# Products of the probabilities with the value rows: one product of 512 columns for P's high half, sums kept unweighted in PSUM's two banks

## The chip, the cores and the metric

The kernel runs on one core of a Trainium2 chip. The metric is the time of one execution on the device in microseconds (us), lower is better. The core has a matrix engine (PE, TensorE), a vector engine (DVE), an activation engine (ACT), a general engine (POOL, GpSimd) and a queue engine (SP) that here issues almost all DMAs. PE writes its sums to PSUM, which has eight banks of 512 f32 columns on 128 partitions; all the others read and write SBUF, and DVE and ACT read PSUM.

## The reference, cut to what matters

One layer of attention on a graph of 4096 nodes with 256 features, after a layer norm:

```
h  = max(layernorm(x), 0)
lQ = masked_x @ Wlq ;  lK = h @ Wlk ;  lV = h @ Wlv + blv
local = where(adj, lQ @ lK.T / 16, -1e9)
le, ge, ee = exp(local - m), exp(global - m), exp(es - m)
denom = sum(le) + ge + ee
res = le/denom @ lV + ge/denom * gV + ee/denom * eV
out = x + max(res, masked_x)
```

`global` and `es` are one number per row, `gV` is one row of 256 values, and `eV = masked_x @ Wev + bev` has a row for each node.

## The kernel before

**Tiling.** The 4096 query rows are taken as 16 row pairs n = 0..15, each of two tiles t = 0, 1 of 128 rows. The 4096 keys are taken as four groups g of 1024. A step p = 4n + g is one block of 2 x 128 rows by 1024 keys. In each step PE makes the scores of block p, and, some six steps later, the products of that block's probabilities with the value rows. All matrix factors are split into a high and a low half in f16, and three of the four products of halves are made: with P the probabilities and V the value rows, P_high·V_high (L1107), P_high·V_low (L1109) and P_low·V_high (L1111), each of 256 columns. `v_rows[:, kc]` holds V_high and V_low of a chunk of 128 keys side by side in 512 columns.

**Order on PE.** It is written out by hand. Up to step 11 a step has four score products (`classic`, banks ps_w, ps_v and twice ps_x) with four chunks of P times V behind each. From step 12 on the scores are made by seven smaller products (`p1`, `p7`, `p5`, `p6`, `p4`, `p2`, `p3`, three instructions of 512 columns each) in a fixed mix with the 16 chunks of P times V. `p_times_v(p, first, last_one)` counts chunks i = 0..15 of step p. Chunks 0 to 7 belong to unit u = 2(p-6)-1 (tile t = 1 of block p-7), chunks 8 to 15 to u + 1 (tile t = 0 of block p-6). So a row pair n opens with chunk 8 of step 4n + 6, its tile t = 0 ends with chunk 15 of step 4n + 9, and its tile t = 1 ends with chunk 7 of step 4n + 10.

**The accumulators.** ps_u has two banks. Row pair n sums into bank n % 2, tile t into the columns t·256 to t·256 + 255. The next row pair uses the other bank, and only from n = 2 on does PE wait for DVE to have read the bank (`s_c1`, from L1100). The last row pair's tile t = 1 sums into ps_w. `ps_u[:, 1, 0:2]` also holds a small sum in step 6 (L1308).

**The other engines' lists** are written out by hand too, step by step. DVE takes the scores out of PSUM (L1476, L1507, L1513, L1519), and has the work that closes a row pair n: `weights` in step 4n + 9, `side_rows` in step 4n + 10 (L1572 and L1575: r12 = blv + w_g·gv + w_e·bev, twice, once per tile), `es_rows` and `local_rows` in step 4n + 11 (L1602; L1587: t_sb = ps_u·r_u + r12), `row_top` in step 4n + 12. ACT makes the masks (L777), the exponentials (L790) and P_high (L814). POOL makes P_low (`p_low`, L611), the low halves of the queries (L596, L591), and the last sum of a row pair (`finish`, L621). SP issues in its own list the transposes of P (L376, L378) and, in step 4n + 13, the store of row pair n (L434). For block slots in SBUF, DVE's take-out of step p waits for the low half of block p-5 (`s_plo`).

Of the kernel before, what the change touches and what calls it, by code (L numbers as in the profile page):

```python
# [24 lines left out]
def build(nc, x, adj, mxT, mx, WlqT, WlkT, Wlv, blv, WgqT, WgkT, Wgv, bgv, Wes, Wev, bev, out):  # L25
# [26 lines left out]
    with ExitStack() as ctx:  # L52
# [6 lines left out]
        def sem(name):  # L59
# [13 lines left out]
        ps_xrow = ps_gv  # L73
        ps_norm = ps_x[:, 0, D:D + 1]
# [111 lines left out]

        eye16 = sb("eye16", [P, 2, P], F16)
# [39 lines left out]
        s_den, s_w, s_e, s_c1, s_c2, s_r, s_fin = (  # L227
            sem(n) for n in ("s_den", "s_w", "s_e", "s_c1", "s_c2", "s_r", "s_fin"))
# [82 lines left out]
        def scale_steps(n):  # L311
            return 3 * min(n, 1) + 3 * min(n, QH) + 5 * max(n - QH, 0)

# [193 lines left out]
        def _(pool):  # L507
# [105 lines left out]

            def finish(n):
# [22 lines left out]
            for p in range(4, NPER + LAG_E):  # L637
# [11 lines left out]
                if live:  # L649
                    p_low(u + 1)  # L650
                if p % NG == 3 and QH <= (p + 5) // NG < NP:
                    mx_low((p + 5) // NG)
# [268 lines left out]
        def _(pe):  # L921
# [156 lines left out]
            def p_times_v(p, first, last_one):  # L1078

                for i in range(first, last_one):  # L1080
# [6 lines left out]
                    if j == 0:  # L1087
# [3 lines left out]
                        if u == LAST + 1:  # L1091
                            pe.wait_ge(s_o11, NPER)
# [9 lines left out]
                    if u >= LAST and t:  # L1102
                        acc = ps_w[:, 0:D]
                    opens = kc == 0 and (t == 0 or u >= LAST)
                    end = kc == T - 1
                    turn = p_turned(u)
                    nc.tensor.matmul(acc, turn[:, 0, j], v_rows[:, kc, 0:D], start=opens, stop=False,  # L1107
                                     skip_group_check=True)
                    nc.tensor.matmul(acc, turn[:, 0, j], v_rows[:, kc, D:2 * D], start=False, stop=False,  # L1109
                                     skip_group_check=True)  # L1110
# [5 lines left out]
            def keys_t3_sum(g):  # L1116

                if g < 2:
                    pe.wait_ge(s_qf, PC - 3)
                else:  # L1120
                    pe.wait_ge(s_c2, 2)
# [135 lines left out]
            for p in range(4, NPER + LAG_V + 1):  # L1257
# [47 lines left out]
                if p == 6:  # L1305
                    pe.wait_ge(s_nrm, 2)
                    pe.wait_ge(s_vlo, T // 2)
                    nc.tensor.matmul(ps_u[:, 1, 0:2], ones32[:, :], nrm[:, :], start=True, stop=True).then_inc(s_nsum, 1)  # L1308
# [5 lines left out]
        def _(dve):  # L1314
# [109 lines left out]
            def weight_scales():  # L1424

                dve.wait_ge(s_nsum, 1)
                nc.vector.tensor_scalar(ncl[:, :], ps_u[:, 1, 0:2], TINY, 2.0 ** -13, ALU.max, ALU.mult).then_inc(s_ncl, 1)
# [115 lines left out]
            def weights(n):  # L1543
                dve.wait_ge(s_exp, 2 * NG * (n + 1))
                dve.wait_ge(s_ge, 2 * (n + 1))
                if n >= 1:
                    dve.wait_ge(s_c2, 2 * n)
                    dve.wait_ge(s_c1, 2 * n)
# [15 lines left out]

# [330 lines left out]
```

## Time and profile before

| | us |
|---|---|
| median of 3 runs | 733.54 |
| lowest and highest run | 733.21 and 733.62 |
| the profiled execution, whole | 734.9 |
| its span on the core | 733.0 |
| granted TensorE clock, mean over the span | 0.998 |

The profile is one execution. Its page begins with the busy time of each engine; other views of the same trace are the groups by line and form, the chain that ended last, the stretches, and the timelines of one engine. Matmuls are pipelined: a record of 0.27 or 0.38 us overlaps the next ones, so what a product costs is read from start to start. Steps of the main part begin after the 12 products of L928 that the chain shows at the end of each fourth step.

### The profile page before, as it was taken

The numbers are of one execution on the slowest core, as the hardware profiler recorded it, in microseconds if no ns is written. First come the engines' busy times: TensorE is split into PE (matmuls) and PEld (weight loads), VectorE is DVE, ScalarE is ACT, GpSimd is POOL, SyncE is SP. The second block draws the span as 40 slices with busy tenths as digits, with TensorE's granted clock in tenths as the row PEclk, the third lists the DMA queues.
The fourth block names the chain that finished last, engine by engine and source line by source line (L and its number), as shares of the span: only waits on it lengthen the run. The fifth ranks groups of instructions, "written<-read, shape, count | busy, mean of one in ns | idle before, by whom it ended". The sixth has DMA issues, their size and how long they took to land.

```text
span 733.0 us, 15029 instructions
## 1 busy us (share of the span) xinstructions
PE 724.1 (99%) x5248; PEld 512.8 (70%) x5248; DVE 563.7 (77%) x1350; ACT 531.9 (73%) x706; POOL 432.4 (59%) x300
## 2 busy tenths in 40 slices
PE   9899999999999999999999999999999999999998
PEld 7667566676766776776767777676777767676787
DVE  6966788868787797878887887878878787876644
ACT  5863876786787677777868687678767777677690
POOL 4779489745555564556445555565556555654583
PEclk9999999999999999999999999999999999999999
DMA  7793586869789897987887798989878798887697
GB/s 243 169 197 61 105 168 160 169 144 204 144 182 168 166 177 142 203 154 176 170 172 158 152 203 142 192 156 178 174 167 163 151 208 148 179 171 174 118 179 166
DMA packets 364716, 121.93 MB, mean 166 GB/s; under 512 B 324832, under 2 KB 364640, under 8 KB 364640
## 3 DMA queue, kind: packets, MB, share of 16 engines
q1 hardware_dynamic: 364096, 120.44, 81.2%
q8 instruction: 42, 0.69, 0.4%
q10 hardware_dynamic: 544, 0.52, 0.2%
q14 instruction: 34, 0.28, 0.1%
HBM read 36.57 MB, written 4.19 MB: 56 GB/s over the span
## 4 chain that ended last, share of the span: by engine, by line
PE 88%; DMA 3%; ACT 2%; POOL 2%; DVE 2%; issue 2%; SPq 0%; DVEq 0%; ACTq 0%; POOLq 0%
PE ps_u L1107 14%; PE ps_u L1111 14%; PE ps_u L1109 14%; PE ps_x L1005 7%; PE ps_x L1004 7%; PE ps_x L1006 7%; PE ps_q L928 4%; PE ps_v L1004 3%; PE ps_v L1006 3%; PE ps_v L1005 3%; PE ps_w L1004 2%; PE ps_w L1005 2%; PE ps_w L1006 2%; PE ps_q L1173 1%; DMA hT<-v_rows 1%
## 5 line engine op out<-in xcount | busy, mean ns | idle before, releaser
L611 POOL TENSOR_TENSOR p_base<-s,p_base 128x1024 f16<-128x1024 f32 x112 | 242.3, 2163 | 227.2 <-ACT p_base L814 213.4
L1107 PE MATMUL ps_u<-v_rows,pT_base 128*128 128x256 f16 x968 | 263.8, 273 | 0.7 <-DMA pT_base<-bias 0.7
L1111 PE MATMUL ps_u<-v_rows,pT_base 128*128 128x256 f16 x968 | 263.8, 273 | 0.0
L1109 PE MATMUL ps_u<-v_rows,pT_base 128*128 128x256 f16 x968 | 263.8, 273 | 0.0
L777 ACT ACTIVATE bias<-adj,big 128x1024 f32<-128x1024 uint8 x127 | 156.5, 1237 | 130.1 <-DVE bmax L1476 126.1
L790 ACT ACTIVATE s<-s,negm,invc 128x1024 f32<-128x1024 f32 x128 | 157.0, 1226 | 6.9 <-DVE negm L1532 6.9
L814 ACT ACTIVATE p_base<-s 128x1024 f16<-128x1024 f32 x122 | 129.0, 1057 | 4.6 <-DMA pT_base<-p_base 0.8
L1107 PEld LDWEIGHTS ps_u<-v_rows,pT_base 128*128 128x128 f16 x968 | 94.7, 98 | 53.2 <-DMA pT_base<-bias 1.0
L1109 PEld LDWEIGHTS ps_u<-v_rows,pT_base 128*128 128x128 f16 x968 | 94.7, 98 | 52.1
L1476 DVE CUSTOM_DVE_ANT_0 s<-ps_x,bias 128x512 f32<-128x512 f32 x128 | 87.1, 685 | 49.6 <-PE ps_x L1006 46.1
L1111 PEld LDWEIGHTS ps_u<-v_rows,pT_base 128*128 128x128 f16 x968 | 94.7, 98 | 11.1
L1005 PE MATMUL ps_x<-hT,qT 128*128 128x512 f16 x152 | 58.1, 382 | 0.0
L1004 PE MATMUL ps_x<-hT,qT 128*128 128x512 f16 x152 | 58.1, 382 | 0.0
L1006 PE MATMUL ps_x<-hT,qT 128*128 128x512 f16 x152 | 58.1, 382 | 0.0
L1519 DVE TENSOR_TENSOR bias<-ps_v,bias 128x512 f32<-128x512 f32 x52 | 36.0, 692 | 26.2 <-PE ps_v L1006 23.4
L1507 DVE TENSOR_TENSOR bias<-ps_x,bias 128x512 f32<-128x512 f32 x52 | 35.8, 688 | 18.6 <-PE ps_x L1006 18.6
L1476 DVE CUSTOM_DVE_ANT_0 s<-ps_w,bias 128x512 f32<-128x512 f32 x64 | 43.7, 684 | 8.1 <-PE ps_w L1006 6.3
L1476 DVE CUSTOM_DVE_ANT_0 s<-ps_v,bias 128x512 f32<-128x512 f32 x64 | 44.0, 687 | 2.4 <-PE ps_v L1006 0.6
L1513 DVE TENSOR_TENSOR bias<-ps_x,bias 128x512 f32<-128x512 f32 x52 | 35.6, 684 | 6.5 <-PE ps_x L1006 6.4
L1575 DVE SCALAR_TENSOR_TENSOR r_base<-bev_b,w,r_base 128x256 f32<-128x256 f32 x30 | 38.8, 1294 | 1.1
L1004 PE MATMUL ps_x<-hW,qT 128*128 128x512 f16 x104 | 39.4, 379 | 0.0
L1005 PE MATMUL ps_x<-hW,qT 128*128 128x512 f16 x104 | 39.4, 379 | 0.0
(242 smaller groups left out, 1266.7 us busy)
## 6 DMA issues: line engine op xcount, KB each, us to landing
adj<-adj SPq DMA_DIRECT2D x64, 256.0 KB, 3.2
pT_base<-p_base SPq DMA_TRANSPOSE x238, 3.3
s<-x SPq DMA_DIRECT2D x7, 512.0 KB, 5.1
f32q<-mx SPq DMA_DIRECT2D x14, 256.0 KB, 3.7
xm<-x SPq DMA_DIRECT2D x14, 256.0 KB, 3.1
xm<-mx SPq DMA_DIRECT2D x14, 256.0 KB, 3.5
out<-t_sb SPq DMA_DIRECT2D x14, 256.0 KB, 2.5
mxT_f<-mxT SPq DMA_DIRECT2D x4, 256.0 KB, 3.2
```

The source lines that it names most:

```text
L611: nc.gpsimd.tensor_tensor(p_rows(u)[:, 1], s32[:, p % NS, u % 2], p_rows(u)[:, 0], ALU.subtract).then_inc(s_plo, 1)
L777: nc.scalar.activation(bias[:, u % NBI].rearrange("p b k -> p (b k)"), adj8[:, p % 2, t], ACT.Identity, bias=big[:, n % 2, 1, t:t + 1], sc ...
L790: nc.scalar.activation(s32[:, p % NS, t], s32[:, p % NS, t], ACT.Exp, bias=negm[:, n % 2, t:t + 1], scale=invc[:, n % 4, t:t + 1], accum_o ...
L814: nc.scalar.activation(p_rows(u)[:, 0], s32[:, p % NS, t], ACT.Copy).then_inc(s_phi, 1)
L1004: nc.tensor.matmul(bank, q_form(n, f, 1), keys(0), start=start, stop=False, skip_group_check=True)
L1005: nc.tensor.matmul(bank, q_form(n, f, 0), keys(1), start=False, stop=False, skip_group_check=True)
L1006: return nc.tensor.matmul(bank, q_form(n, f, 0), keys(0), start=False, stop=stop, skip_group_check=True)
L1107: nc.tensor.matmul(acc, turn[:, 0, j], v_rows[:, kc, 0:D], start=opens, stop=False, skip_group_check=True)
L1109: nc.tensor.matmul(acc, turn[:, 0, j], v_rows[:, kc, D:2 * D], start=False, stop=False, skip_group_check=True)
L1111: done = nc.tensor.matmul(acc, turn[:, 1, j], v_rows[:, kc, 0:D], start=False, stop=end, skip_group_check=True)
L1476: nc.vector.tensor_tensor_reduce(out=s32[:, p % NS, t, b * BLOCK:(b + 1) * BLOCK], in0=bank, in1=bias[:, u % NBI, b], scale=1.0, scalar=-3 ...
L1575: nc.vector.scalar_tensor_tensor(r12[:, t], bev_b[:, :], w3[:, t, 1:2], r12[:, t], ALU.mult, ALU.add).then_inc(s_r, 1)
```

## The change

P_high times `v_rows[:, kc]`, all 512 columns, is one instruction (L1132 in the changed kernel) where two of 256 columns stood; V_high and V_low products of one tile then lie side by side in one whole bank, and P_low·V_high (L1134) adds to the first half. Each tile t now owns bank t of ps_u, for every row pair, so the next row pair's tile t uses the same bank. DVE has a new helper `value_rows(n, t)`: it copies the second half of the bank to t_sb (L1597) and adds the first half (L1599); this gives `s_c1`, for which PE waits before chunk 8 of step 4n + 10 (t = 0) and before chunk 0 of step 4n + 11 (t = 1), from n = 0 on. `value_rows` also waits for the previous row pair's store, since it writes t_sb. `local_rows` (L1619) now reads t_sb where it read PSUM, and counts on `s_c3`. The last row pair keeps the three products of 256 columns. `side_rows` moves to POOL for n = 1 to 13, as eight instructions (L627, L628, L630, L632 for each tile); it stays on DVE for n = 0 and 14. The small sum of step 6 moves to the last two columns of ps_q.

```diff
+            def side_rows(n, t):                     # on POOL
+                k = side_steps(n) + 3 * t
+                pool.wait_ge(s_w, n + 1)
+                pool.wait_ge(s_c3, 2 * n - 1 + t)
...
+                nc.gpsimd.tensor_scalar(r12[:, t], gv_b[:, :], w3[:, t, 0:1], None, ALU.mult).then_inc(s_rstep, 1)
+                nc.gpsimd.tensor_scalar(side_e[:, :], bev_b[:, :], w3[:, t, 1:2], None, ALU.mult).then_inc(s_rstep, 1)
...
+                nc.gpsimd.tensor_tensor(r12[:, t], r12[:, t], side_e[:, :], ALU.add).then_inc(s_rstep, 1)
...
+                nc.gpsimd.tensor_tensor(r12[:, t], r12[:, t], blv_b[:, :], ALU.add).then_inc(s_r, 1)
...
-                            if n >= 2:
-                                pe.wait_ge(s_c1, 2 * (n - 1))
-                    acc = ps_u[:, n % 2, t * D:(t + 1) * D]
...
+                        if g == 0 and n >= 1:
+                            pe.wait_ge(s_c1, 2 * (n - 1) + t + 1)
+                    acc = ps_u[:, t, 0:D]
...
+                        nc.tensor.matmul(ps_u[:, t], turn[:, 0, j], v_rows[:, kc], start=kc == 0, stop=False,
+                                         skip_group_check=True)
...
+            def value_rows(n, t):
+
+                dve.wait_ge(s_pv, 2 * NG * n + 2 * NG - 1 + t)
...
+                    dve.wait_ge(s_out, 16 * n)
+                nc.vector.tensor_copy(t_rows(n)[:, t], ps_u[:, t, D:2 * D]).then_inc(s_c0, 1)
+                dve.wait_ge(s_c0, 2 * n + t + 1)
+                nc.vector.tensor_tensor(t_rows(n)[:, t], ps_u[:, t, 0:D], t_rows(n)[:, t], ALU.add).then_inc(s_c1, 1)
...
-                    nc.vector.scalar_tensor_tensor(t_rows(n)[:, t], ps_u[:, n % 2, t * D:(t + 1) * D], r_u[:, t:t + 1],
-                                                   r12[:, t], ALU.mult, ALU.add).then_inc(s_c1, 1)
+                    nc.vector.scalar_tensor_tensor(t_rows(n)[:, t], t_rows(n)[:, t], r_u[:, t:t + 1], r12[:, t], ALU.mult,
+                                                   ALU.add).then_inc(s_c3, 1)
...
                     out11(p)
                     if p == 4:
                         v_low(T // 2 - 1)
+                    if p == 10:
+                        value_rows(0, 0)
                     out12(p)
...
                     out21(p)
+                    if p == 10:
+                        value_rows(0, 1)
                     out22(p)
```

**PE, second half of step 10,** where row pair 1 opens. Before (the first three rows are the end of a score product, then chunk 8):

```order
L1004 MATMUL ps_x<-hT,qT 128x512
L1005 MATMUL ps_x<-hT,qT 128x512
L1006 MATMUL ps_x<-hT,qT 128x512
L1107 MATMUL ps_u<-v_rows,pT_base 128x256 [waits s_pT_low2,s_pT2]
L1109 MATMUL ps_u<-v_rows,pT_base 128x256
L1111 MATMUL ps_u<-v_rows,pT_base 128x256
```

After:

```order
L1028 MATMUL ps_x<-hT,qT 128x512
L1029 MATMUL ps_x<-hT,qT 128x512
L1030 MATMUL ps_x<-hT,qT 128x512
L1132 MATMUL ps_u<-v_rows,pT_base 128x512 [waits s_c1,s_pT_low2,s_pT2]
L1134 MATMUL ps_u<-v_rows,pT_base 128x256
```

The chunk has two instructions where it had three, and its first one now waits for `s_c1`, DVE's reading of the bank.

**DVE, from the end of `weights(0)` through step 10.** L1476 (L1501 after) takes a score block out of ps_w, ps_v or ps_x. Before:

```order
L1557 TENSOR_SCALAR r_u<-rden,v_unit 128x2 [waits s_vunit,s_den]
L1558 TENSOR_TENSOR w<-mass,rden 128x4
L1476 ISA s,bmax<-ps_w,bias 128x512 [waits s_plo,s_bias,s_p2]
L1476 ISA bmax 128x1
L1476 ISA s,bmax<-ps_v,bias 128x512 [waits s_plo,s_bias,s_p3]
```

After:

```order
L1582 TENSOR_SCALAR r_u<-rden,v_unit 128x2 [waits s_vunit,s_den]
L1583 TENSOR_TENSOR w<-mass,rden 128x4
L1501 ISA s,bmax<-ps_w,bias 128x512 [waits s_plo,s_bias,s_p2]
L1501 ISA bmax 128x1
L1597 COPY t_sb<-ps_u 128x256 [waits s_pv]
L1599 TENSOR_TENSOR t_sb<-ps_u,t_sb 128x256 [waits s_c0]
L1501 ISA s,bmax<-ps_v,bias 128x512 [waits s_plo,s_bias,s_p3]
```

The copy and the sum of tile t = 0 of row pair 0 stand behind step 10's first take-out, which itself waits for `s_plo`.

**POOL, step 14,** a step in which a row pair's side rows are due. Before, one P_low follows the other:

```order
L611 TENSOR_TENSOR p_base<-s,p_base 128x1024 [waits s_pT_low1,s_phi]
L596 TENSOR_TENSOR q_hl<-f32q,q_hl 128x896 [waits s_qhi]
L611 TENSOR_TENSOR p_base<-s,p_base 128x1024 [waits s_pT_low2,s_phi]
L611 TENSOR_TENSOR p_base<-s,p_base 128x1024 [waits s_pT_low0,s_phi]
```

After (the second tile's four rows, alike but for a wait for `s_r`, are left out here):

```order
L616 TENSOR_TENSOR p_base<-s,p_base 128x1024 [waits s_pT_low2,s_phi]
L627 TENSOR_SCALAR r_base<-gv_b,w 128x256 [waits s_rstep,s_c3,s_w]
L628 TENSOR_SCALAR side_e<-bev_b,w 128x256
L630 TENSOR_TENSOR r_base<-r_base,side_e 128x256 [waits s_rstep]
L632 TENSOR_TENSOR r_base<-r_base,blv_b 128x256 [waits s_rstep]
```

Eight instructions of 256 columns now stand between this step's last P_low and the next step's first one.

## Rows read from the trace of the kernel before

**Rows 1.** page, part 1: busy us, share of span and instructions by engine.

```profile
PE 724.1 (99%) x5248; PEld 512.8 (70%) x5248; DVE 563.7 (77%) x1350; ACT 531.9 (73%) x706; POOL 432.4 (59%) x300
```

**Rows 2.** view by stretches: length, busy us (instructions) by engine, granted clock, DMA.

```profile
400.00:500.00 100.00, 100.00 (x721) 70.36 (x720) 79.71 (x182) 75.72 (x97) 55.07 (x35) 1.00 0.86 165
```

**Rows 3.** chain that ended last: start us, length us, what and how many.

```profile
151.16 1.73 PE ps_q L1123 x8
...
284.44 1.34 PE ps_q L928 x12
...
310.86 1.31 PE ps_q L928 x12
...
326.17 1.34 PE ps_q L928 x12
```

**Rows 4.** timeline of PE (start, length, instruction) where row pair 1 begins.

```profile
130.59 0.38 PE L1006 MATMUL ps_x<-hT,qT 128*128 128x512 f16 x1
130.81 0.27 PE L1107 MATMUL ps_u<-v_rows,pT_base 128*128 128x256 f16 x1
```

**Rows 5.** timelines of DVE and POOL at that place, same columns.

```profile
131.32 1.93 DVE L1557 TENSOR_SCALAR r_u<-rden,v_unit 128x2 f32<-128x2 f32 x1
...
133.40 0.69 DVE L1476 CUSTOM_DVE_ANT_0 s<-ps_w,bias 128x512 f32<-128x512 f32 x1
...
134.01 0.08 DVE L1476 DVE_READ_ACCUMULATOR2_ANT bmax<- 128x1 f32 x1
...
131.10 2.13 POOL L611 TENSOR_TENSOR p_base<-s,p_base 128x1024 f16<-128x1024 f32 x1
```

**Rows 6.** timeline of PE and two stretches, where the clock fell.

```profile
36.04 0.39 PE L1004 MATMUL ps_v<-hT,qT 128*128 128x512 f16 x1 [1.63 <-DMA hT<-v_rows]
...
36.00:42.00 6.00, 5.96 (x28) 3.12 (x29) 4.96 (x16) 3.65 (x8) 3.73 (x3) 0.72 1.10 238
38.00:39.00 1.00, 1.00 (x3) 0.30 (x2) 1.00 (x3) 1.00 (x3) 0.00 (x0) 0.50 0.78 252
```

**Rows 7.** timelines of DVE and PE, opening of step 19.

```profile
220.96 2.23 DVE L1575 SCALAR_TENSOR_TENSOR r_base<-bev_b,w,r_base 128x256 f32<-128x256 f32 x1
...
223.12 0.68 DVE L1476 CUSTOM_DVE_ANT_0 s<-ps_v,bias 128x512 f32<-128x512 f32 x1
...
223.47 0.27 PE L1111 MATMUL ps_u<-v_rows,pT_base 128*128 128x256 f16 x1
223.86 0.39 PE L1004 MATMUL ps_v<-hW,qT 128*128 128x512 f16 x1
```

**Rows 8.** timelines of POOL and DVE in step 39.

```profile
436.39 2.13 POOL L611 TENSOR_TENSOR p_base<-s,p_base 128x1024 f16<-128x1024 f32 x1 [5.14 <-ACT p_base L814]
...
438.70 2.14 POOL L611 TENSOR_TENSOR p_base<-s,p_base 128x1024 f16<-128x1024 f32 x1 [0.18 <-ACT p_base L814]
...
440.07 0.88 DVE L1587 SCALAR_TENSOR_TENSOR t_sb<-ps_u,r_u,r_base 128x256 f32<-128x256 f32 x2
```

**Rows 9.** timelines: a store, all stores' landing, PE in step 26.

```profile
293.73 0.58 SPq L434 DMA_DIRECT2D out<-t_sb  x1
...
DMA to landing us min/median/max: 2.4/2.6/4.6
...
300.59 0.27 PE L1107 MATMUL ps_u<-v_rows,pT_base 128*128 128x256 f16 x1
```

**Rows 10.** groups by line and form: busy us, mean ns, idle before.

```profile
L1587 DVE SCALAR_TENSOR_TENSOR t_sb<-ps_u,r_u,r_base 128x256 f32<-128x256 f32 x28 | 12.2, 476 | 0.0
...
L582 POOL TENSOR_TENSOR f32q<-f32q 128x128 f32<-128x128 f32 x13 | 5.9, 456 | 16.6 <-ACT f32q L729 16.6
...
L621 POOL TENSOR_TENSOR t_sb<-t_sb,xm 128x512 f32<-128x512 f32 x14 | 17.8, 1270 | 0.0
```

**Rows 11.** timeline of DVE at the end.

```profile
727.27 0.49 DVE L1854 SCALAR_TENSOR_TENSOR s<-ps_u,r_u,adj 128x256 f32<-128x256 f32 x1 [5.33 <-PE ps_u L1111]
```

More of the change, by code:

```diff
@@ L73, in build @@
         ps_xrow = ps_gv
+        ps_tops = ps_q[:, 1, 2 * D - 2:2 * D]
         ps_norm = ps_x[:, 0, D:D + 1]
@@ L226, in build @@
         s_exp, s_ge, s_phi, s_plo, s_pv = (sem(n) for n in ("s_exp", "s_ge", "s_phi", "s_plo", "s_pv"))
-        s_den, s_w, s_e, s_c1, s_c2, s_r, s_fin = (
-            sem(n) for n in ("s_den", "s_w", "s_e", "s_c1", "s_c2", "s_r", "s_fin"))
+        s_den, s_w, s_e, s_c0, s_c1, s_c2, s_c3, s_rstep, s_r, s_fin = (
+            sem(n) for n in ("s_den", "s_w", "s_e", "s_c0", "s_c1", "s_c2", "s_c3", "s_rstep", "s_r", "s_fin"))
         s_nrm, s_nsum, s_ncl, s_nscale, s_unw, s_mwhi, s_mwlo, s_wvhi, s_wvlo = (
@@ L650, in _ @@
                     p_low(u + 1)
+                n = (p - 10) // NG
+                if p % NG == 2 and 1 <= n < NP - 2:
+                    side_rows(n, 0)
+                    side_rows(n, 1)
                 if p % NG == 3 and QH <= (p + 5) // NG < NP:
@@ L1306, in _ @@
                     pe.wait_ge(s_nrm, 2)
+                    pe.wait_ge(s_qf, 7)
                     pe.wait_ge(s_vlo, T // 2)
-                    nc.tensor.matmul(ps_u[:, 1, 0:2], ones32[:, :], nrm[:, :], start=True, stop=True).then_inc(s_nsum, 1)
+                    nc.tensor.matmul(ps_tops, ones32[:, :], nrm[:, :], start=True, stop=True).then_inc(s_nsum, 1)
                 n = p // NG + 1
@@ L1780, in _ @@
                         weights((p - 9) // NG)
-                    if step == 2 and p >= 10:
-                        side_rows((p - 10) // NG, 0)
-                        side_rows((p - 10) // NG, 1)
+                    if p == 10:
+                        side_rows(0, 0)
+                        side_rows(0, 1)
                     if step == 3 and p >= 11:
@@ L1793, in _ @@
                         add11(p)
+                    if step == 2 and ended:
+                        value_rows(done, 0)
                     if wino(old):
@@ L1799, in _ @@
                         q_rows(m)
-                    if step == 2 and ended:
+                    if step == 2 and (done == NP - 2 or PC == 8 and done == 0):
                         side_rows(done, 0)
@@ L1812, in _ @@
                         out21(old)
+                    if step == 2 and ended:
+                        value_rows(done, 1)
                     if p == NPER:
@@ L1823, in _ @@
                         q_row_scales(m)
-                    if step == 2 and ended:
+                    if step == 2 and (done == NP - 2 or PC == 8 and done == 0):
                         side_rows(done, 1)
```

62 lines of the change are left out of this document (34 added, 28 removed).

## The prediction

> **What bounds the kernel now.** I read four views in this order. The page's busy times first: PE works 724.1 of 733.0 us, DVE 563.7, ACT 531.9, POOL 432.4 [rows 1]. A share over the whole span can hide waits, so the view by stretches next: from 400 to 500 us PE is busy for 100.00 of 100.00 us at full granted clock (1.00, that is 2.4 GHz) while DVE is busy for 79.7 and POOL for 55.1 [rows 2]. The chain of waits says the same in time: the 12 query products that close every fourth step start at 284.44 and 326.17, so four steps take 41.73 us, and there is no other engine in between [rows 3]. In the main part PE alone sets the pace. It follows that an instruction taken from PE is gained in full, work on DVE or POOL costs nothing until PE waits for it, and each wait of PE is lost in full. The fourth view is the timeline of the engines at each place where the change gives PE something new to wait for.
>
> **PE's products: a gain of 2.2 us.** The change puts 512 columns in one instruction for 2 x 256. Twelve products of 256 columns take 1.31 us, 0.1092 each, and twelve of 258 take 1.34 [rows 3]. Four steps hold 84 score products of 512 columns, 192 P·V products of 256, and those two groups of twelve. 41.73 - 1.31 - 1.34 - 192 x 0.1092 leaves 18.11 us for the 84, so 0.2156 each. Eight of the same width in a row took 1.73, 0.2163 each [rows 3]. A pair thus costs 0.2183 and the wide one 0.2156 to 0.2163: the columns pass at the same rate, and only some 2.0 to 2.7 ns for one instruction less are saved. I take 2.5, since the main loop is where it happens. Fewer products also means fewer weight loads, but those lie beside the products already and bring nothing more. How many count: each of row pairs 0 to 14 has 64 chunks. Those of row pair 0 lie ahead of the wait of the next paragraph and are swallowed by it. Of row pair 14 only 30 come before the last scores, whose chain through exponential, P_low and transposes sets the end from there. So 13 x 64 + 30 = 862 chunks x 2.5 ns = 2.2 us (1.7 to 2.3).
>
> The Trainium skill ("TensorE: Matmul & The Clock Gate", section "Back-to-back issue gap") gives N/2.4 + 2.5 ns for a gap at full clock, which these rows bear out at both widths. The same section says that in a real stream a product of 512 columns takes about 131 ns; the 84 score products in this very stream take 216 [rows 3], so the measurement decides.
>
> **PE's new wait in step 10: a loss of 4.2 us.** Before, row pair 1 opened in a bank that nobody had used. Now its first product, chunk 8 of step 10, writes bank 0, and waits for DVE's copy and sum of row pair 0. PE reaches that product at 130.81, right behind a score product [rows 4]. DVE is not there: its list has `weights(0)`, whose small L1557 starts at 131.32 and takes 1.93 us because POOL holds its two-operand P_low from 131.10 to 133.23, and then step 10's first take-out, which needs the slot that the same P_low frees. That starts at 133.40 and DVE is free at 134.01 [rows 5]. Only there do copy and sum come. Neither form stands in the trace; the nearest is L1587, 256 columns from PSUM with a second operand, 476 ns [rows 10]. Two of them end near 134.96; each could be 0.1 shorter. PE goes on at 135.0 and has lost 135.0 - 130.8 = 4.2 us (4.0 to 4.3). Nothing that leads to 133.40 depends on the change. What is queued behind the waiting product on PE is everything, the score products of steps 10 and 11 included; since DVE and ACT are late themselves there, they catch up while PE stands. Nothing later makes up for it, because PE works without a gap from there to the end of the scores. So this step, once in the run, costs more than all the products gain.
>
> **PE's clock behind that wait: a loss of 1.7 us.** In the opening stage PE once stood idle for 1.63 us before 36.04, behind a string of one-column products. Then the granted clock was 0.50 (1.2 GHz) from 38 to 39, and 0.72 over the six us from 36 to 42, with PE busy [rows 6]: 6 x 0.28 = 1.7 us of full-speed work lost. The new idle time is over twice as long. I expect the same fall once, 1.7 us; the bounds are 0 (the clock holds) and 3.4 (twice as long).
>
> **The same waits in the later row pairs: nothing.** In steps 4n + 10 DVE gets to `value_rows(n, 0)` right behind its first take-out, early in the step, and what it can wait for is the store of row pair n - 1. The slowest store shows how much is left: issued at 293.73, landed 4.6 later at 298.3, and copy and sum would end at 299.3, where PE comes to chunk 8 of step 26 at 300.59 [rows 9]: 1.3 us to spare; the median landing is 2.6, with 3.3 to spare. For t = 1 PE's next use of the bank is a further half step away. The two copies and two sums add 4 x 0.48 = 1.9 us to DVE in this step, and the four side-row instructions that leave it take 0.48 at best and 2.23 where POOL is in the way [rows 7], so the take-outs of scores come no later than now.
>
> **Side rows.** In one place they hold PE now: L1575 at 220.96 takes 2.23 us, the take-out behind it starts at 223.12, and PE, which needs that bank, goes from 223.47 to 223.86 where 0.11 is usual [rows 7]. That wait goes: 0.3 us gained. What is late next there is nothing within a us. On POOL eight instructions of 256 columns come instead. 128 columns take 456 ns and 512 take 1270 [rows 10], so 256 take about 0.73 with two operands; with one operand I bound them by 0.46. Eight make 4.7 us (3.7 to 5.8). The next P_low starts at 436.39 behind 5.14 us of idle time [rows 8]: they fit, or run over by under a us, and the P_low of unit 2(p - 5) is used a whole step (10.4 us, [rows 3]) after it is made. Cost nothing; without that cover it would be up to 0.7 us for each of 13 row pairs.
>
> **`local_rows` from SBUF.** L1587 reads PSUM and takes 0.48 each, undisturbed, though POOL runs a P_low from 438.70 to 440.84 beside it at 440.07 [rows 8]. The new form reads two operands from SBUF, like the side rows: in [rows 7] such an instruction lasts until POOL's is over. The two can so end 1.4 us later than 440.95, and the take-out behind them at about 443.0. PE comes to that bank in step 40 after p1, p7 and four chunks, 2.6 us; the step begins at 441.6 (the next query products at 451.36, three periods after 326.17 in [rows 3], less 9.77 for 21 and 48 products), so at 444.2. Cost nothing, with a margin of about a us. The Trainium skill ("SBUF — State Buffer", section "Who interferes with whom") states the same as an exclusive lock for a whole instruction; by that rule the margin stays positive too.
>
> **The end.** The last product of P·V is not touched, and DVE waits for PE for 5.33 us before its last sums [rows 11], so DVE's longer list there is covered.
>
> **The sum.** +4.2 (wait) + 1.7 (clock) - 2.2 (products) - 0.3 (old wait) = +3.4 us. The profiled execution took 734.9 whole, 733.0 in span, so it would be 738.3 and 736.4. It was 1.4 above the median of the runs; from that median, 733.54, I predict 736.9.
>
> **The rivals.**
> *The clock holds.* The wait comes, but the idle time falls so that the granted clock stays at 1.00, as it did in short gaps elsewhere: 733.54 + 4.2 - 2.2 - 0.3 = 735.2. For it speaks that PE is busy on both sides of the gap; against it that 1.63 us did it once [rows 6]. The same page of the Trainium skill, part 1, has half clock as the idle state, which agrees with that row.
> *PE never waits in step 10.* Then only the gains remain: 733.54 - 2.5 = 731.0, faster. It decides itself on DVE's copy and sum being done by 130.8, 4.2 us sooner than I read; for that the take-out in front of them must not be held until 133.23, against [rows 5].
> *The store holds DVE in each row pair.* `value_rows` waits for the previous store, which in [rows 9] leaves 1.3 us. If stores land later than 5.9 us after issue, each further us costs PE one, 14 times over; 0.3 us on average is 4 more: 741.
> *The wide product is cheaper than its columns.* If PE overlapped it so that it cost what a narrow one does, 0.109 would go 862 times: 94 us, 643. The score products of the same width deny it [rows 3]. The 131 ns of the Trainium skill, same section as above, point this way.
>
> **How the numbers follow.** Forecast (736 to 739 with the bounds of the clock) 62 in 100; clock holds 19; store or `local_rows` holding PE repeatedly 10; no wait 8; wide product cheap 1. A difference of 0.2%, 1.5 us, is about what a measurement of this kernel can tell from none. Slower than 735.0 are the forecast, the repeated waits, and most of the 735.2 case, 0.84; faster are the two last, 0.09; 0.07 are left for between. The range holds the first two and some of the repeated waits: 734.6 to 740.0.
>
> **What would show it.** In the profile after: PE idle about 4.2 us near 131, released by DVE's sum; a stretch of granted clock 0.50 behind it; four steps in 41.73 - 0.16 = 41.57 us; no PE wait near 223; POOL's side rows ending by the next P_low; PE 100 of 100 us busy later. I am wrong if PE does not stand at 131, if four steps are not shorter, or if a small wait comes back in each row pair.

## The result and the profile after

The changed kernel takes 770.5 us (median of 4 runs, 769.58 to 774.68), the kernel before 733.43 beside it: 1.051 times as long, 95% interval 1.0492 to 1.0528. The prediction said 736.9 and slower. The direction is right, the size is not: 37.1 us were lost, not 3.4. The profiled execution took 769.58 us, 767.8 of them span.

The first lines are from the page of the changed kernel (busy us, share, instructions by engine; then the chain that ended last), and answer to [rows 1]. The stretch under them is that of [rows 2], with two short ones behind long waits; its columns are busy us by engine, granted clock, DMA share and GB/s.

```profile
span 767.8 us, 13250 instructions
PE 732.7 (95%) x4288; PEld 419.3 (55%) x4288; DVE 559.7 (73%) x1358; ACT 529.8 (69%) x706; POOL 513.6 (67%) x404
...
POOL 31%; PE 24%; issue 19%; DVE 13%; ACT 7%; DMA 4%; DVEq 0%; SPq 0%; POOLq 0%; ACTq 0%
...
400.00:500.00 100.00, 96.86 (x539) 52.67 (x538) 72.97 (x177) 72.40 (x93) 69.91 (x55) 0.98 0.82 163
134.00:140.00 6.00, 6.00 (x25) 2.75 (x24) 2.74 (x8) 3.03 (x4) 1.49 (x1) 0.72 0.57 122
376.00:380.00 4.00, 4.00 (x13) 1.62 (x13) 2.46 (x6) 3.97 (x5) 0.43 (x1) 0.58 0.79 173
```

PE no longer sets the pace alone: it is busy for 96.86 of 100 us, and POOL has the largest share of the chain, 31%. The busy figure hides part of the loss, since PE counts as busy while it runs at half clock. The pace itself is best read from the twelve query products of every fourth step, which [rows 3] used. In the changed kernel's timeline of PE two of them, four row pairs (sixteen steps) apart, stand at

```profile
427.15 1.50 PE L952 MATMUL ps_q<-m_base,mxT_f 128*128 128x258 f16 x12
...
604.27 1.50 PE L952 MATMUL ps_q<-m_base,mxT_f 128*128 128x258 f16 x12
```

so four steps take (604.27 - 427.15) / 4 = 44.28 us where they took 41.73 [rows 3]. That is 2.55 us for each row pair here. Thirteen at this rate would be 33 of the 37.1 us (an estimate; the ninth run below gives 31.6), and most of the rest is in step 10. The view of waits names what PE waited for (us in total, times, longest):

```profile
PE ps_v L1028 <- DVE bmax L1501: 19.4, 17, 2.3
PE ps_u L1132 <- DVE t_sb L1599: 4.2, 1, 4.2
PE ps_x L1028 <- DVE bmax L1501: 2.1, 1, 2.1
```

The second line is the wait of step 10 that was predicted. The first was not: 17 waits on the take-out (L1501) of the score bank ps_v. One of the long ones, in the timelines of PE, DVE and POOL at 376 us (start, length, engine, line, in brackets the idle time before it and who ended it):

```profile
373.10 0.38 PE L1132 MATMUL ps_u<-v_rows,pT_base 128*128 128x512 f16 x1
373.32 0.27 PE L1134 MATMUL ps_u<-v_rows,pT_base 128*128 128x256 f16 x1
375.89 0.39 PE L1028 MATMUL ps_v<-hW,qT 128*128 128x512 f16 x1 [2.31 <-DVE bmax L1501]
...
377.71 0.63 PE L1132 MATMUL ps_u<-v_rows,pT_base 128*128 128x512 f16 x1
...
371.74 0.69 DVE L1501 CUSTOM_DVE_ANT_0 s<-ps_w,bias 128x512 f32<-128x512 f32 x1 [1.66 <-POOL p_base L616]
...
372.36 2.87 DVE L1619 SCALAR_TENSOR_TENSOR t_sb<-t_sb,r_u,r_base 128x256 f32<-128x256 f32 x2
375.15 0.68 DVE L1501 CUSTOM_DVE_ANT_0 s<-ps_v,bias 128x512 f32<-128x512 f32 x1
...
362.36 0.94 POOL L627 TENSOR_SCALAR r_base<-gv_b,w 128x256 f32<-128x256 f32 x1
...
368.75 0.73 POOL L632 TENSOR_TENSOR r_base<-r_base,blv_b 128x256 f32<-128x256 f32 x1
369.44 4.21 POOL L616 TENSOR_TENSOR p_base<-s,p_base 128x1024 f16<-128x1024 f32 x2
373.62 1.33 POOL L596 TENSOR_TENSOR q_hl<-f32q,q_hl 128x512 f16<-128x512 f32 x1
```

Read from the bottom. POOL works on side rows from 362.36 to 369.48, 7.1 us, so the next P_low (L616) starts at 369.44 instead of waiting for ACT as it did in [rows 8]. DVE's take-out of ps_w needs a slot that the first of these two P_low frees and starts at 371.74. Right behind it in DVE's list stand the two `local_rows` (L1619), which read two operands from SBUF. They meet the second P_low and then L596 on POOL, and take 2.87 us for two where [rows 8] has 0.88. The take-out of ps_v stands behind them, and PE, ready at 373.43, gets the bank at 375.89: 2.46 us lost. Behind it the granted clock falls: the wide product at 377.71 lasts 0.63 where the same form took 0.38 at 373.10, and from 376 to 380 the clock is 0.58, which is 4 x 0.42 = 1.7 us more. The waits come in a pattern of 0.83, 0.48 and 2.45 us over two row pairs: 3.76 + 1.7 = 5.5, close to the 5.4 us by which eight steps, 88.56 us, exceed twice 41.57.

The waits of 0.83 stand behind the same `local_rows` (2.88 us for two at 327.80). Those of 0.48 do not: there the take-out of ps_v stands behind another DVE instruction that meets a P_low on POOL, one on two columns with one operand. The rows are from the timelines of DVE, POOL and PE:

```profile
348.30 1.91 DVE L1429 TENSOR_SCALAR invc<-rpow 128x2 f32<-128x2 f32 x1
...
351.90 0.68 DVE L1501 CUSTOM_DVE_ANT_0 s<-ps_v,bias 128x512 f32<-128x512 f32 x1
...
348.06 2.13 POOL L616 TENSOR_TENSOR p_base<-s,p_base 128x1024 f16<-128x1024 f32 x1 [0.55 <-ACT p_base L838]
...
352.64 0.39 PE L1028 MATMUL ps_v<-hW,qT 128*128 128x512 f16 x1 [0.32 <-DVE bmax L1501]
```

### The profile page after: what moved, and what is told of

Same layout as the page of the kernel before. It is cut to its first block, busy times and chain, and to the rows that moved or that the text cites. A ratio compares the mean times of both kernels' runs of the same rounds, so it can differ in the third digit from the quotient of the medians.

```text
span 767.8 us, 13250 instructions
## 1 busy us (share of the span) xinstructions
PE 732.7 (95%) x4288; PEld 419.3 (55%) x4288; DVE 559.7 (73%) x1358; ACT 529.8 (69%) x706; POOL 513.6 (67%) x404
## 4 chain that ended last, share of the span: by engine, by line
POOL 31%; PE 24%; issue 19%; DVE 13%; ACT 7%; DMA 4%; DVEq 0%; SPq 0%; POOLq 0%; ACTq 0%
POOL p_base L616 17%; PE ps_u L1132 5%; PE ps_u L1134 3%; POOL r_base L627 3%; POOL side_e L628 3%; ACT s L814 3%; POOL r_base L630 2%; ACT p_base L838 2%; DVE s L1501 2%; PE ps_x L1028 2%; DVE p_base L1565 2%; POOL q_hl L601 2%; PE ps_x L1029 2%; DVE invc L1429 2%; PE ps_x L1030 1%
## 5 line engine op out<-in xcount | busy, mean ns | idle before, releaser
L616 POOL TENSOR_TENSOR p_base<-s,p_base 128x1024 f16<-128x1024 f32 x112 | 238.8, 2138 | 184.4 <-ACT p_base L838 179.2
L1132 PE MATMUL ps_u<-v_rows,pT_base 128*128 128x512 f16 x960 | 338.0, 384 | 4.2 <-DVE t_sb L1599 4.2
L1134 PE MATMUL ps_u<-v_rows,pT_base 128*128 128x256 f16 x976 | 268.6, 275 | 0.0
L1132 PEld LDWEIGHTS ps_u<-v_rows,pT_base 128*128 128x128 f16 x960 | 94.6, 99 | 120.0 <-issue 8.9
L1134 PEld LDWEIGHTS ps_u<-v_rows,pT_base 128*128 128x128 f16 x976 | 96.3, 99 | 53.6 <-issue 1.4
L1501 DVE CUSTOM_DVE_ANT_0 s<-ps_x,bias 128x512 f32<-128x512 f32 x128 | 87.4, 686 | 49.7 <-PE ps_x L1030 38.0
L1501 DVE CUSTOM_DVE_ANT_0 s<-ps_w,bias 128x512 f32<-128x512 f32 x64 | 44.0, 687 | 44.6 <-POOL p_base L616 38.5
L1501 DVE CUSTOM_DVE_ANT_0 s<-ps_v,bias 128x512 f32<-128x512 f32 x64 | 43.9, 685 | 7.1 <-PE ps_v L1030 5.7
L1028 PE MATMUL ps_x<-hW,qT 128*128 128x512 f16 x104 | 40.8, 392 | 2.1 <-DVE bmax L1501 2.1
L1029 PE MATMUL ps_x<-hW,qT 128*128 128x512 f16 x104 | 40.7, 391 | 0.0
L1030 PE MATMUL ps_x<-hW,qT 128*128 128x512 f16 x104 | 40.7, 391 | 0.0
L1619 DVE SCALAR_TENSOR_TENSOR t_sb<-t_sb,r_u,r_base 128x256 f32<-128x256 f32 x28 | 39.0, 1433 | 0.0
L1028 PE MATMUL ps_v<-hW,qT 128*128 128x512 f16 x52 | 19.9, 383 | 19.5 <-DVE bmax L1501 19.4
```

Of the source, the lines that this page charges most:

```text
L616: nc.gpsimd.tensor_tensor(p_rows(u)[:, 1], s32[:, p % NS, u % 2], p_rows(u)[:, 0], ALU.subtract).then_inc(s_plo, 1)
L1028: nc.tensor.matmul(bank, q_form(n, f, 1), keys(0), start=start, stop=False, skip_group_check=True)
L1029: nc.tensor.matmul(bank, q_form(n, f, 0), keys(1), start=False, stop=False, skip_group_check=True)
L1030: return nc.tensor.matmul(bank, q_form(n, f, 0), keys(0), start=False, stop=stop, skip_group_check=True)
L1132: nc.tensor.matmul(ps_u[:, t], turn[:, 0, j], v_rows[:, kc], start=kc == 0, stop=False, skip_group_check=True)
L1134: done = nc.tensor.matmul(acc, turn[:, 1, j], v_rows[:, kc, 0:D], start=False, stop=end, skip_group_check=True)
```

## The experiments

Two theories stood at the start. **Late P_low**: POOL's side rows are longer than the pause they were put in, and DVE and PE are paced by POOL. **Standing behind POOL**: DVE's operations with two SBUF operands last until POOL's instruction is over, and hold what is queued behind them. A third, that the product of 512 columns costs more than its columns, stands in the expectation of the first run, and the sixth answers it. The ratio of each run is to the kernel before on the same chip.

**1. Side rows back on DVE, all else of the change kept.**

```
-                n = (p - 10) // NG
-                if p % NG == 2 and 1 <= n < NP - 2:
-                    side_rows(n, 0)
-                    side_rows(n, 1)
...
-                    if step == 2 and (done == NP - 2 or PC == 8 and done == 0):
+                    if step == 2 and ended:
                         side_rows(done, 0)
```

> The changed kernel with the side rows back on DVE in every row pair (four instructions, as in the kernel before); all else as changed. Theory 1 (the eight POOL instructions, 7.1 us together, push P_low of the next step back and the take-outs of scores wait for it): the waits that come back in each row pair go, what stays is the one wait and clock fall of step 10, so 733.4 + 4.2 + 1.7 - 2.5 = 737. Theory 2 (local_rows with two SBUF operands, or the value rows on DVE, hold PE): nothing much changes, 765 to 770. Theory 3 (the product of 512 columns costs more than its columns): 765 to 770 too, with four steps longer than 41.7 us without a wait in them.

Measured: 744.72 us, ratio 1.0153 (1.0137 to 1.0169). 26 us of the 37 are gone, so POOL's side rows are needed for the large loss; but 11.3 stay where 3.6 were expected. 5.9 of them are step 10, as expected (wait 4.2, clock 0.72 over six us). Against them stands the product's gain, and the rest are waits of 0.5 to 1.1 us on ps_v, once per row pair. Two rows of DVE's timeline show their cause, in a row pair where PE is held from 440.55 to 441.07:

```profile
436.80 1.34 DVE L1604 SCALAR_TENSOR_TENSOR r_base<-gv_b,w,blv_b 128x256 f32<-128x256 f32 x1
438.18 2.23 DVE L1607 SCALAR_TENSOR_TENSOR r_base<-bev_b,w,r_base 128x256 f32<-128x256 f32 x1
440.33 0.68 DVE L1497 CUSTOM_DVE_ANT_0 s<-ps_v,bias 128x512 f32<-128x512 f32 x1
```

The side rows have two SBUF operands too. Behind the copy and sum of the value rows they now meet a P_low (437.81, 2.31 us). This is the disturbance of [rows 7], which the change was predicted to remove.

From the second row pair on, `local_rows`, with its two SBUF operands, holds PE nowhere in this run. It is stretched nearly as much as in the changed kernel (group mean 1242 ns against 1433), but it starts early enough. The rows are from the timelines of DVE and PE:

```profile
448.17 2.60 DVE L1615 SCALAR_TENSOR_TENSOR t_sb<-t_sb,r_u,r_base 128x256 f32<-128x256 f32 x2
450.69 0.68 DVE L1497 CUSTOM_DVE_ANT_0 s<-ps_v,bias 128x512 f32<-128x512 f32 x1
...
452.12 0.38 PE L1024 MATMUL ps_v<-hW,qT 128*128 128x512 f16 x1
```

The take-out is over at 451.37 and PE comes at 452.12 without a wait: a margin of 0.75 us.

**2. The first run, plus `value_rows(0, 0)` moved from step 10 to the end of step 9.**

> As e1_side_on_dve, and the copy and sum of row pair 0, tile 0, are done by DVE at the end of step 9, ahead of weights(0), instead of behind the first take-out of step 10. If the reading of step 10 holds, PE no longer waits there and the clock stays: 737 - 5.9 = 731.1, faster than the kernel before by 2.3 us (0.3%). If the wait in step 10 had another releaser, it stays at 737. If early value rows only move the wait to the opening of step 12 (DVE's list is late there by 0.9 us more), 731.5 to 733.

Measured: 740.64 us, 1.0097 (1.0083 to 1.0112), 4.1 less than the first where 5.9 less were expected. The 4.2 us wait is gone and the clock stays at 1.00, but a second wait was hidden behind the first: tile 1's value rows stand behind another take-out that waits for POOL. The row is from PE's timeline:

```profile
136.91 0.38 PE L1128 MATMUL ps_u<-v_rows,pT_base 128*128 128x512 f16 x1 [1.68 <-DVE t_sb L1595]
```

**3. The kernel before, with POOL's side rows alone.** The products, take-out and `local_rows` (one operand from PSUM) are those of before; DVE keeps side rows only for row pairs at the two ends.

> The kernel before with one part of the change alone: the side rows of row pairs 1 to 13 on POOL, as the changed kernel has them. Products, banks and local_rows (from PSUM) are as before. Theory 1 (late P_low): most of the loss is here, 750 or more. Theory 2 (the lock on local_rows) expects none of it: 733 to 735.

Measured: 741.75 us, 1.0115 (1.0099 to 1.0130). Neither number: late P_low costs something by itself, but a fifth of the loss. PE waits twice per row pair, 0.33 to 0.41 us each:

```profile
PE ps_v L1027 <- DVE bmax L1499: 5.1, 21, 0.5
```

Here DVE's `local_rows` stands in the same place behind the same late take-out, and takes its usual 0.87 for two (group mean 477 ns). So 0.4 us is what a late P_low costs with the short form, and up to 2.45 with the form that stands behind POOL. The two kernels differ in the value rows on DVE as well, so the operand's share alone is read from the timelines and was not run by itself.

**4. The changed kernel with POOL's eight side-row instructions cut to 128 of 256 columns.**

> The changed kernel with the eight POOL instructions cut to 128 of 256 columns (the side rows of the other columns are left out, so part of the output is missing). They should take about 0.48 and 0.46 us each, 3.9 us together, and fit the 5.1 us that POOL has free before the next P_low. Theory 1: 737 to 739, as e1. Theory 2: the number of columns on POOL changes little, 765 or more.

Measured: 748.93 us, 1.0211 (1.0195 to 1.0226), and this run is the best test of the prediction's arithmetic. In POOL's timeline the eight lasted from 402.23 to 406.93:

```profile
402.23 0.60 POOL L627 TENSOR_SCALAR r_base<-gv_b,w 128x128 f32<-128x128 f32 x1
...
406.47 0.46 POOL L632 TENSOR_TENSOR r_base<-r_base,blv_b 128x128 f32<-128x128 f32 x1
406.90 2.12 POOL L616 TENSOR_TENSOR p_base<-s,p_base 128x1024 f16<-128x1024 f32 x1
```

That is 4.7 us, exactly the length the prediction had given them at full width. With that length the kernel is still 15.5 us slower than before, 9.6 more than the 5.9 of step 10. So the wrong price of the side rows is only part of the error. P_low is still late, too: it starts 1.7 us behind the start of the twelve query products at 405.17, where it was 0.5 before, since POOL comes to its side rows later.

**5. Side rows of tile 0 on DVE, of tile 1 on POOL, and both value rows of row pair 0 ahead of step 10's take-outs.**

> The changed kernel with both value rows of row pair 0 taken early (tile 0 at the end of step 9, tile 1 ahead of step 10's third take-out), and the side rows split: tile 0 on DVE (two instructions, where POOL is idle), tile 1 on POOL (four, 3.4 us). POOL has 5.1 us free there. If the late P_low comes only from POOL's list being longer than its free time, all waits of PE in the later row pairs go: 731 to 732. If any side row on POOL holds the take-outs, or local_rows behind P_low holds PE, 737 to 745.

Measured: 744.21 us, 1.0143 (1.0114 to 1.0173). The waits of step 10 are down to 0.3 us and the clock is 1.00, but a new wait of 1.1 us stands at 147.40 (the same as in the eleventh run, below). And PE waits 0.8 and 0.5 us in each row pair. The first of them is new. The rows are from DVE's and POOL's timelines:

```profile
439.89 0.69 DVE L1472 TENSOR_REDUCE mmax<-f32q 128x2 f32<-128x512 f32 x1 [1.66 <-DMA f32q<-mx]
440.61 1.61 DVE L1474 TENSOR_SCALAR mcl<-mmax 128x2 f32<-128x2 f32 x1
442.25 2.08 DVE L1476 TENSOR_SCALAR mscale<-mcl 128x2 int32<-128x2 int32 x1
...
440.06 4.25 POOL L616 TENSOR_TENSOR p_base<-s,p_base 128x1024 f16<-128x1024 f32 x2
```

Two DVE instructions on two columns, one operand each, that take 0.17 and 0.29 us in the changed kernel's own timeline at 367.37 and 367.57 take 1.61 and 2.08 here, each until one of the two P_low of POOL is over. POOL's first P_low is not late here: it starts 0.45 us behind the start of the twelve query products at 439.61, and before it started at 436.39 [rows 8], 0.49 behind those at 435.90. DVE is late: before, the same reduction ran at 434.71, here it waited until 439.89 for the transfer of mx. Why that transfer comes later was not tested.

**6 and 7. Another way to sum: value rows are weighted when they leave PSUM, `local_rows` is gone for n >= 1, side rows are on DVE with tile 1 a step later, both early value rows; once with the wide product (6), once with two products of 256 columns in its place (7).**

```
-                        nc.tensor.matmul(acc, turn[:, 0, j], v_rows[:, kc, 0:D], start=kc == 0, stop=False,
+                        nc.tensor.matmul(ps_u[:, t], turn[:, 0, j], v_rows[:, kc], start=kc == 0, stop=False,
...
-                            nc.tensor.matmul(ps_u[:, t, D:2 * D], turn[:, 0, j], v_rows[:, kc, D:2 * D], start=False,
-                                             stop=False, skip_group_check=True)
```

> Products of 512 columns, row pair 0 early as in e5_split_side, but from row pair 1 on the value rows are weighted as they leave PSUM (r12 = second half of the bank * r_u + blv, then + first half * r_u, both with one operand from PSUM), es_rows writes t_sb, local_rows falls away, and the four side-row instructions are on DVE, tile 1's a step later, where POOL is idle. DVE has two instructions fewer per row pair than e1_side_on_dve and only the side rows read two SBUF operands. If PE has no wait left, 731.0, 2.4 us below the kernel before. If the products of 512 columns bring nothing, 733.4. If waits of 0.5 us stay, 737.

> As e6_weighted_values, with two products of 256 columns where it has one of 512; nothing else differs. By the rows of the kernel before, a pair costs 2.0 to 2.7 ns more, over 896 chunks 1.8 to 2.4 us: 733.2 if e6 is 731.0. If the wide product is no cheaper, both are the same.

Measured: 733.76 us, 0.9994 (0.9977 to 1.0011), and 734.78, 1.0016 (1.0002 to 1.0029). The 37 us are gone with the wide product kept, so the wide product has no part in them. The medians differ by 1.0 us in the expected direction, less than the 2.2 expected, and both stay above the 731 and 733.2 of the expectation. Part of it can be read. Where no wait is in the way, four steps take 41.58 us in six (query products at 283.46 and 325.04) and 41.74 in seven (450.26 and 492.00), with nothing else altered: the 0.16 us that the prediction gave the product. But six has a wait of 1.1 us at 147.34 that seven has not, one of 1.38 at 719.55, and 0.36 to 0.43 in three places.

**8. The changed kernel with POOL's full side rows; for n >= 1 the last sum reads ps_q and t_sb in the place of `es_rows`.** One operand from PSUM, and nothing between the take-outs of ps_w and ps_v. The weighting of the local sums is left out.

> The changed kernel, side rows on POOL and all, but local_rows of row pairs 1 to 14 takes its first operand from ps_q in PSUM and its second from t_sb, at the place of es_rows, instead of t_sb and r12 from SBUF (the weighting of the local sums is so left out for these rows). The count of DVE instructions is the same. If what e3 doesn't explain (770.5 - 741.8, less 3.4 for step 10 and the products) is DVE standing behind POOL in local_rows, this gives 745 to 750. If it is the extra value rows on DVE or the late P_low alone, 765 or more.

Measured: 738.33 us, 1.0061 (1.0038 to 1.0083), where both theories expected 745 or more. POOL's side rows are as long as in the changed kernel. The P_low behind them starts 2.3 us behind the start of the twelve query products (402.06 and 399.75), where it was 0.5 before and is 2.5 and 4.1 by turns in the changed kernel. So it is as late as in every second row pair there, and the steps are at full speed: the query products stand 166.3 us apart over four row pairs, 41.58 for each four steps. A late P_low with nothing between the two take-outs costs nothing that the steps show, so late P_low as the cause by itself falls here. But two things were altered, the operand and the place, and the next run alters the place alone.

**9. The changed kernel, complete, with `local_rows` moved behind the take-out of ps_v and two more DVE operations.**

```
+                    if step == 0 and 16 <= p <= NPER:
+                        local_rows((p - 12) // NG)
                     if p < NPER:
                         add22(p)
...
-                    if step == 3 and ended:
+                    if step == 3 and ended and p > NPER:
                         local_rows(done)
```

> The changed kernel with one move: local_rows of row pairs 1 and up stands behind the take-out of ps_v, the copies of the next block's first chunks (two more DVE operations), not ahead of it. POOL's side rows, P_low and all operands stay. Theory A (VectorE stands behind POOL in the operations with two SBUF operands, and that is what holds the take-out of ps_v): of the waits of 2.45, 0.85 and 0.48 us per two row pairs the first goes, and with it the 1.7 us of clock behind each: (2.45 + 1.7) x 5.5 = 23 us, so about 747; a little less gain if the 2.9 us stand now ahead of another bank. Theory B (the late P_low alone holds the take-out, whose wait for the same step's P_low stays): the wait moves with P_low, 765 to 770.

Measured: 738.87 us, 1.0063 (1.0047 to 1.0080). Moving two instructions past three operations gives back 31.6 us. No other instruction is changed. The rows are from DVE's and POOL's timelines:

```profile
362.55 0.69 DVE L1501 CUSTOM_DVE_ANT_0 s<-ps_w,bias 128x512 f32<-128x512 f32 x1 [1.06 <-POOL p_base L616]
...
363.17 0.69 DVE L1501 CUSTOM_DVE_ANT_0 s<-ps_v,bias 128x512 f32<-128x512 f32 x1
...
366.13 0.88 DVE L1619 SCALAR_TENSOR_TENSOR t_sb<-t_sb,r_u,r_base 128x256 f32<-128x256 f32 x2
...
360.25 4.22 POOL L616 TENSOR_TENSOR p_base<-s,p_base 128x1024 f16<-128x1024 f32 x2
364.43 1.16 POOL L596 TENSOR_TENSOR q_hl<-f32q,q_hl 128x512 f16<-128x512 f32 x1
367.59 4.70 POOL L616 TENSOR_TENSOR p_base<-s,p_base 128x1024 f16<-128x1024 f32 x2 [2.00 <-ACT p_base L838]
```

The take-out of ps_w still waits for POOL, 1.06 us, and PE does not notice. `local_rows` now falls into POOL's pause from 365.59 to 367.59 and takes 0.88 for two, with the same two SBUF operands. Its group mean over the run is 546 ns; in the changed kernel it was 1433. My expectation was 747 by the one theory: it counted only the waits of 2.45 us, while those of 0.83 and 0.48 went too. No run leaves `local_rows` in its old place in the changed kernel with one operand from PSUM; the nearest is the third, with 0.4 us.

**10. The eighth run with both early value rows.**

> The kernel of e8 (local sums unweighted: the weighting of t_sb is left out and the local row is ps_q times weight plus t_sb) with both value rows of row pair 0 ahead of the take-outs of step 10. Expected: 738.3 - 4.2 - 1.7 = 732.4, with steps of 41.58 us per row pair, no wait of TensorE at step 10 and the clock at 1.00 there. That would close the account of the changed kernel: product - 1.6, start 0, tail about + 1. A rival: something late at step 11 to 13 keeps 1 to 2 us, 734.

Measured: 733.57 us, 0.9994 (0.9982 to 1.0005), 4.8 less than the eighth.

**11. The ninth run with both early value rows: the complete computation.**

> e9 with both value rows of row pair 0 ahead of the take-outs of step 10. If the opening and the row pairs add up as separate losses: e9 less 4.2 to 5.9 us, so near 742. If the opening's wait only shifts POOL and VectorE against each other and is taken back, e9's time.

Measured: 733.52 us, 0.9989 (0.9977 to 1.0002), 5.35 less than the ninth. The opening and the row pairs are separate losses and add up: 31.6 + 5.35 = 36.95 of 37.1 us. The sum is net: the product's gain is in it, and so are two waits that the kernel before has not (below). The rows are a stretch of this kernel and its twelve query products, in PE's timeline:

```profile
400.00:500.00 100.00, 100.00 (x570) 55.65 (x569) 71.61 (x187) 75.04 (x96) 69.86 (x52) 1.00 0.83 168
...
410.20 1.50 PE L952 MATMUL ps_q<-m_base,mxT_f 128*128 128x258 f16 x12
...
576.51 1.50 PE L952 MATMUL ps_q<-m_base,mxT_f 128*128 128x258 f16 x12
```

PE is busy for 100.00 of 100 us at full clock again, with POOL at 69.86, and four steps take (576.51 - 410.20) / 4 = 41.58 us.

**12. The eleventh with the side rows back on DVE, tile 1's a step later.**

> e11 with the side rows back on VectorE, tile 0's in the step of the value rows and tile 1's a step later. All four changed places are then out of the way of POOL: wide products, unweighted take-out, local_rows later. Expected 731 to 733 if nothing else is late (product - 2.2 against 733.4); 735 to 737 if VectorE behind POOL in local_rows (1.2 us each) holds a bank 0.3 to 0.5 us once a row pair.

Measured: 734.99 us, 1.0007 (0.9995 to 1.0019). No better than with POOL's side rows: the wait at 148 us stays, and small waits of 0.2 to 0.44 us come back in some row pairs. None of the twelve beats the kernel before by more than can be told.

## Why the prediction was wrong, step by step

**The product: right.** A wide product with its partner in a slot of 0.2156 for 0.2183 was to bring four steps from 41.73 to 41.57. The eighth, ninth, tenth and eleventh runs have 41.58, and the sixth and seventh, which differ in the product alone, 41.58 and 41.74. The Trainium skill ("TensorE: Matmul & The Clock Gate", section "Back-to-back issue gap") has 131 ns for a product of 512 columns in a stream; the changed kernel's L1132, 0.22 apart from L1134 at 373.10 and 373.32, goes against it.

**The wait of step 10 and the clock behind it: right.** 4.2 us predicted, and the row shows

```profile
133.38 0.38 PE L1132 MATMUL ps_u<-v_rows,pT_base 128*128 128x512 f16 x1 [4.20 <-DVE t_sb L1599]
```

with a clock of 0.72 over six us behind it, the predicted 1.7. The ninth and eleventh runs differ by 5.35 where the sum said 5.9, and the eleventh has a wait of 1.1 us at 148.50 that the ninth has not. The new forms L1597 and L1599 took 416 and 424 ns; 476 was assumed.

**Side rows on POOL, "cost nothing": wrong in price and in what it said of the cover.** The price: one-operand instructions were bounded by 0.46. The groups of the changed kernel say (busy us, mean ns)

```profile
L627 POOL TENSOR_SCALAR r_base<-gv_b,w 128x256 f32<-128x256 f32 x26 | 24.1, 928 | 2.6 <-POOL r_base L632 2.6
L628 POOL TENSOR_SCALAR side_e<-bev_b,w 128x256 f32<-128x256 f32 x26 | 24.1, 926 | 0.0
L630 POOL TENSOR_TENSOR r_base<-r_base,side_e 128x256 f32<-128x256 f32 x26 | 19.0, 729 | 2.2
```

so the one-operand form costs 0.93, more than the 0.73 of two operands, which was right. Eight make 7.1 us, beyond both the 5.8 that the prediction bounded them by and the 5.14 of the pause. I had taken the value of a form that no row showed from the idea that fewer operands cost less; no row excluded more. The cover: "the P_low is used a whole step after it is made" holds for PE's use. DVE's take-outs wait for the same P_low, because it frees their slot. The prediction had used that very wait in step 10, [rows 5], and had not asked whether it stands in every step. It stands in every step's list, and before it had mostly been met in time (3.6 us in 2 waits). In the changed kernel DVE waited for POOL's P_low 47.7 us in 39 waits.

**`local_rows`, "a margin of about a us": the step that failed.** Its mechanism was right, an operation with two SBUF operands lasts until POOL's is over, and even the place was right, the take-out of ps_v. But the margin was reckoned with POOL as in [rows 8], and the same change moves POOL. Before, `local_rows` began 4.0 us ahead of PE's need, at 440.07 [rows 8], and PE came at

```profile
444.06 0.38 PE L1004 MATMUL ps_v<-hW,qT 128*128 128x512 f16 x1
```

With POOL left where it was, the reckoning holds: the first run has 2.60 us for the two and a margin of 0.75. In the changed kernel `local_rows` began at 372.36, 1.1 ahead of 373.43. The sum then is short: 1.07 - 2.87 + 0.08 for the overlap of two instructions - 0.68 for the take-out - 0.06 = -2.46, the wait that was read. With a `local_rows` of 0.88 the same sum gives -0.47, near the 0.33 to 0.41 of the third run. The two edits were each costed against the kernel before, with the other one left out. Each alone costs little: POOL's side rows 8.3 us (third run), the operands of `local_rows` nothing that PE shows from the second row pair on (first run; its other 5.4 us, 11.3 less 5.9 and net of the product's gain, stand behind side rows on DVE where the rows were read). Together they cost 31.6. The Trainium skill ("SBUF — State Buffer", section "Who interferes with whom") says that who issues first gets the shared ports for a whole instruction and that the other blocks. The rows agree for one order of issue: at 372.36 POOL's second P_low was already running, and DVE's two instructions took 2.87 us; in the ninth run POOL paused, and the same two took 0.88.

**The old wait at 223.86, "gone": partly.** In the changed kernel there are longer ones in its place. In the eleventh run none over 0.3 stands between 190 and 242. At 242.80 a new one of 0.98 comes, once: the query products wait for a transfer of q_hl. POOL's L596, which feeds it, stands behind the side rows and starts at 235.50, where before it started at 231.93; the transfer is issued at 238.20 for 236.35 and takes 5.6 us to land for 3.7. Nothing in the prediction spoke of it.

**What is left of the gain.** With all four places cleared, the prediction's terms say 733.4 - 2.2 = 731.2 and the eleventh run measured 733.5. In the profiles, from the query products near 243 to PE's last product, it takes 485.2 us against 487.0 before: 1.8 gained there, as reckoned. Up to there 1.35 are lost on balance. Two new waits make more than that, the 0.98 at 242.80 and 1.1 at 148 us, with rows from the timelines of DVE and PE of the eleventh run:

```profile
139.66 2.24 DVE L1611 SCALAR_TENSOR_TENSOR r_base<-bev_b,w,r_base 128x256 f32<-128x256 f32 x1
...
142.33 2.23 DVE L1611 SCALAR_TENSOR_TENSOR r_base<-bev_b,w,r_base 128x256 f32<-128x256 f32 x1
...
148.50 0.38 PE L1028 MATMUL ps_x<-hT,qT 128*128 128x512 f16 x1 [0.82 <-DVE bmax L1501]
```

The side rows of row pair 0 are on DVE, and with the value rows moved ahead they meet two P_low on POOL; the ninth run has 0.48 for each at 141.18 and 142.09, and no such wait. The 1.8 gained less the 1.35 lost leave 0.5 by span (732.5 against 733.0), within what the runs scatter, so whether the eleventh is faster at all stays open.

**The rivals.** The third, a hold of PE repeated in each row pair, came nearest, with chance 10 in 100, but its price, 4 us, was worked out for the store. The range ended at 740.0, since a margin of "about a us" was counted as cover rather than as a quantity with an error that thirteen row pairs multiply. The two price bounds that should have widened it, 5.8 for POOL against 5.14 of pause, stood in the text and got "0.7 us for each of 13", 9 us, that the range left out.

## What to carry to other kernels

When a change loads one engine and makes another engine's instructions depend on when that engine is busy, cost the two together: shift the first engine's timeline by the added work, and only then read what the second meets. A margin of one us in a step that repeats thirteen times is not a margin but the first candidate for the bound. When a queue holds an instruction that can be stretched by a neighbour, look at what stands behind it: moving two such instructions past three operations was worth 31.6 us here.

## What the runs showed of the hardware

- POOL's `tensor_scalar` with one f32 operand takes 928 ns at 256 columns and 605 at 128; `tensor_tensor` takes 729 and 456. The Trainium skill ("GPSIMD Engine Reference", section "4.1 Engine selection") calls POOL some 2x slower than DVE "for 2-input ops" and has "1-input is roughly line-rate". Here the one-input form with a scalar is the slower one on POOL, and DVE copies the same 256 columns, out of PSUM, in 416 ns.
- DVE instructions of two columns with one operand stand behind POOL too: 1.61 and 2.08 us for 0.17 and 0.29 (fifth run), 1.91 for L1429 in the changed kernel.
- Behind each of PE's five waits of 2.45 us in the changed kernel (idle 2.31 at 375.89), products took 0.43 us start to start, the granted clock's level of 1.2 GHz; behind those of 0.83 and 0.48 the stretches show no fall. The length of a wait does not tell it alone. In the same trace idle times of 1.85 us before 242.66 and 2.07 before 728.32 left the clock at 1.00, and so did 1.68 in the second run; at 36 us the clock fell behind 1.63 [rows 6] and stayed at 1.00 behind 1.79 in the changed kernel.
